# Two places of a twelve-sublayer kernel: four PSUM slots handed out by expected release, and one batch of keys made a stage early

## The reference

```python
for i in range(DEPTH):                                            # 6
    x = attn_layer(shift_tokens(x), Wqkv[i], q_scale[i], k_scale[i], Wo[i]) + x
    x = ffn_layer(shift_tokens(x), ln_g[i], ln_b[i], W1[i], b1[i], W2[i], b2[i]) + x
# attn_layer: q, k, v = x @ Wqkv; q, k l2-normed, scaled, rotated; softmax over 64 keys; @ Wo
# ffn_layer: layer norm, a * gelu(gate), W2
```

```python
h = _mha(x, x, x, Wq1, bq1, Wk1, bk1, Wv1, bv1, Wo1, bo1, causal=True)
out = _mha(h, encoder_k, encoder_v, Wq2, bq2, Wk2, bk2, Wv2, bv2, Wo2, bo2, causal=False)
# _mha: q = x @ Wq + bq, k, v alike; softmax(q k^T / sqrt(8)) v; @ Wo + bo
```

## Time and profile before

| | us |
|---|---|
| median of 3 runs | 4151.44 (4146.84 to 4154.14) |
| the profiled execution, its own time | 4158.42 |
| its span, first to last instruction | 4156.6 |
| local transformer, from 2440 to 3405 | 965 |
| first attention of the double one, from 3464 to 3579 | 115 |
| second attention, from 3579 to 4094 | 515 |

### The profile page before, as it was taken

One profiled execution on the slowest core, in us unless ns is written; L12 is line 12 of the kernel. 1 busy time (PEld: TensorE's weight loads), 2 busy tenths in 40 slices (PEclk: granted clock), 3 DMA queues, 4 the chain that ended last, 5 costly groups with the idle time before them and its releaser, 6 DMA issues. The chain is left out here.

```text
span 4156.6 us, 96204 instructions
## 1 busy us (share of the span) xinstructions
PE 3506.0 (84%) x40492; PEld 2405.1 (58%) x40492; DVE 2612.0 (63%) x4495; ACT 1970.9 (47%) x3518; POOL 1271.6 (31%) x844
## 2 busy tenths in 40 slices
PE   7575888999999996799778668888888878799996
PEld 4455656777777776433232446666666656466674
DVE  5124485666666663688775857777777757556563
ACT  1132345555555553588711235555555544255552
POOL 1102205555555544100030445555555521000000
PEclk9586799999999997999889779999999999699996
DMA  1022300000000006200001021111111101000000
GB/s 39 5 68 74 124 27 11 9 1 9 1 1 1 1 1 210 95 1 1 4 1 44 24 71 42 34 46 52 34 46 36 27 17 36 12 17 19 11 2 11
DMA packets 88438, 131.27 MB, mean 32 GB/s; under 512 B 18290, under 2 KB 59946, under 8 KB 87244
## 3 DMA queue, kind: packets, MB, share of 16 engines
q1 hardware_dynamic: 85004, 118.89, 10.1%
q0 software_dynamic: 3008, 6.23, 0.4%
HBM read 86.37 MB, written 10.94 MB: 23 GB/s over the span
## 5 line engine op out<-in xcount | busy, mean ns | idle before, releaser
L2196 ACT ACTIVATE narrow_probsT<-narrow_ps_t 128x512 f32<-128x512 f32 (+1 forms) x448 | 233.3, 568 | 224.9 <-PE narrow_ps_t L2110 222.4
L2686 POOL TENSOR_TENSOR wide_probs<-wide_probs,wide_factor 128x1024 f32<-128x1024 f32 x128 | 239.7, 1894 | 311.5 <-ACT wide_factor L2647 311.5
L175 POOL TENSOR_TENSOR model_Y<-model_Y,model_X 128x512 f32<-128x512 f32 x12 | 15.2, 1269 | 1029.7 <-POOLq L66 1029.7
L2643 ACT ACTIVATE wide_probs<-wide_ps_s,wide_nm 128x1024 f32<-128x1024 f32 (+1 forms) x256 | 237.7, 929 | 172.2 <-DVE wide_nm L2728 152.7
L3098 PE MATMUL bonds_ps<-bonds_act_of,bonds_out 128*32 128x448 f32 (+3 forms) x1024 | 284.3, 573 | 25.1 <-ACT bonds_rows L3081 18.6
L2248 DVE TENSOR_REDUCE narrow_part<-narrow_ps_s 128x1 f32<-128x512 f32 x384 | 236.1, 685 | 105.1 <-PE narrow_ps_s L2093 105.1
L3808 POOL TENSOR_TENSOR local_turn<-local_turn 128x1024 f32<-128x1024 f32 x96 | 226.4, 2367 | 225.9 <-DVE local_turn L3866 225.9
L2110 PE MATMUL narrow_ps_t<-narrow_Q,second_KQ 32*128 32x256 f32 (+1 forms) x1664 | 291.5, 410 | 3.0 <-ACT narrow_probsT L2196 3.0
L2093 PE MATMUL narrow_ps_s<-second_KQ 32*128 32x512 f32 x768 | 255.7, 674 | 35.0 <-DMA second_KQ<-narrow_close 16.9
L2723 DVE TENSOR_REDUCE wide_nm<-wide_ps_s 128x1 f32<-128x1024 f32 x128 | 156.0, 1219 | 193.7 <-PE wide_ps_s L2529 193.7
L3047 DVE TENSOR_TENSOR bonds_strain<-peri_in_moved 128x1664 f32<-128x1664 f32 (+3 forms) x128 | 257.5, 2088 | 7.0 <-ACT bonds_act_of L3070 6.0
(11 more groups left out here) (629 smaller groups left out, 8412.9 us busy)
## 6 DMA issues: line engine op xcount, KB each, us to landing
moe_w<-in_L_ffn_w SPq DMA_DIRECT2D x62, 512.0 KB
local_V<-local_V SPq DMA_DIRECT2D x96, 128.0 KB
e_wqkv<-in_L_ffn_qkv SPq DMA_DIRECT2D x6, 1536.0 KB, 7.3
local_V<-local_V SPq DMA_DIRECT2D x144, 64.0 KB
context_rows<-in_ctx SPq DMA_DIRECT2D x8, 768.0 KB
e_keys<-in_ctx_T SPq DMA_DIRECT2D x6, 800.5 KB, 4.5
second_KQ<-narrow_close SPq DMA_DIRECT2D x64, 58.0 KB
e_source<-in_ctx_T SPq DMA_DIRECT2D x4, 800.5 KB, 4.4
```

What stands on the lines that cost most here:

```text
L2196: act.activation(probsT[0:high, c % PROBS, h, 0:wide], bank[0:high, 0:wide], ACT.Exp).then_inc(t_taken_act.sem, 1)
L2643: act.activation(probs[:, n % 2, h, lo:hi], ps_s[h][:, 0:hi - lo], ACT.Exp, bias=nm[:, n % 2, h, 2 * half:2 * half + 1], scale=1.0, accum_ ...
L2686: pool.tensor_tensor(v, v, factor[:, n // 4 % 2, j:j + 1].broadcast_to([P, CUT]), ALU.mult).then_inc(lowered[i].sem, 1)
```

## The change

Two edits that don't touch each other.

In the local transformer a slot is chosen by a small plan: with a guess of how long PE makes each kind (`MAKES`) and how long its reader holds it (`HOLDS`), each unit takes the slot that comes free first, and waits for that slot's last user (`last_in`). DVE's sum of the probabilities becomes an event "inv" of its own, behind v (gv) and ahead of s.

In the double attention the keys of batch 0 of the second part are made in steps 6 to 9 of the first, one piece a step ("ahead"), and spread by SP behind them. Its queries of batch 0 are no longer packed and spread: four products with weights that the host has already padded to the spread layout ("query", 256 columns each) give them, and ACT writes them into `KQ`. The padded weights lie in the tile `O`, which isn't in use yet. SP's first reload of the context waits for nothing but its reading, and DVE's start waits for `top` alone (in all three calls of the function).

```diff
@@ early_narrow
+        early.close = early.sbuf("close", [P, K + T])
+        early.O = early.sbuf("O", [P, 2, TB, D])
+        early.first_q = early.O[:, :, :, :].rearrange("p k t d -> p (k t) d")
+        early.load(early.first_in, early.first_q, m.dram[a.name + "_first_q"])
+        early.load(early.first_in, early.first_cols[:, :], m.dram[a.name + "_first_cols"])
@@ narrow_attention, the order
+    AHEAD = (6, 7, 8, 9)
+    AHEAD_UNITS = [(0, 512), (512, 1024), (1024, 1536), (1536, S)]
...
-                for n in range(len(project_units)):
-                    put(N * s - (8 * (len(project_units) - n) + 12 if s else 18 - 4 * n), 7, "project", s, n)
+                for n in range(2 if s == 0 else 0):
+                    put(N * s - (18 - 4 * n), 7, "query", s, n)
+                for n in range(len(project_units) if s else 0):
+                    put(N * s - (8 * (len(project_units) - n) + 12), 7, "project", s, n)
...
+            if following is not None and s in AHEAD:
+                events.append((at, 3.5, "ahead", s, AHEAD.index(s)))
@@ SP
+                side, nth = taken_t(("ahead", AHEAD[-1], len(AHEAD) - 1))
+                sp.wait_ge(side.sem, side.nth(nth))
+                for g in range(G):
+                    for h in range(H):
+                        at = DH * (H * g + h)
+                        sp.dma_start(following.KQ[32 * h:32 * h + DH, 0, g, 0:S], following.close[at:at + DH, 0:S]).then_inc(following.first_K_in.sem, 16)
...
+                sp.wait_ge(source_read.sem, source_read.nth(1))
+                sp.dma_start(source[:, 0, :], m.dram["ctx_T"][2]).then_inc(source_in[0].sem, 16)
+                for b in range(1, B):
@@ POOL
             pool.memset(top[:, :, :, :], 0.0)
+            pool.drain().then_inc(top_cleared.sem, 1)
@@ PE
+                if kind == "ahead":
...
+                    pe.matmul(bank[:, 0:c1 - c0], following.qk[:, 0, P:], following.source[:, 0, c0:c1], start=True, stop=True).then_inc(made.sem, 1)
+                elif kind == "query":
...
+                    for j in range(2):
+                        mm = pe.matmul(bank[:, j * T:(j + 1) * T], early.first_q[:, 2 * n + j, :], qsrc[:, 0:T], start=True, stop=True, skip_group_check=True)
...
-                        pe.wait_ge(KQ_in[b % 2].sem, KQ_in[b % 2].nth(0, b // 2 + 1))
+                        wait_keys(pe, b)
+                        if b == 0:
+                            side, nth = taken_t(("query", 0, 1))
+                            pe.wait_ge(side.sem, side.nth(nth))
@@ ACT
+                    act.activation(following.close[:, c0:c1], bank[:, 0:c1 - c0], ACT.Identity, bias=following.cols[:, 1:2]).then_inc(t_taken_act.sem, 1)
...
+                        ins = act.activation(KQ[:, 0, i, K:], bank[:, j * T:(j + 1) * T], ACT.Identity, bias=early.first_cols[:, i:i + 1], scale=-scale)
@@ DVE
-            dve.wait_ge(cleared.sem, cleared.nth(1))
+            if a.context:
+                dve.wait_ge(early.first_in.sem, early.first_in.nth(32))
+                dve.tensor_scalar(early.first_cols[:, :], early.first_cols[:, :], -scale, None, ALU.mult).then_inc(scaled.sem, 1)
+            dve.wait_ge(top_cleared.sem, top_cleared.nth(1))
@@ local_layers, rounds(): odd and even round
-                            ("root", r), ("v", r), ("gv", shift), ("s", r - 1), ("rest", r), ("wo", r - 3), ("o", r - 2), ("gx", shift)]
+                            ("root", r), ("v", r), ("gv", shift), ("inv", r - 2), ("s", r - 1), ("rest", r), ("wo", r - 3), ("o", r - 2), ("gx", shift)]
...
-                            ("s", r - 1), ("rest", r), ("wo", r - 3), ("o", r - 2), ("sh", (r - 4) // 2)]
+                            ("inv", r - 2), ("s", r - 1), ("rest", r), ("wo", r - 3), ("o", r - 2), ("sh", (r - 4) // 2)]
@@ local_layers, slots
+    MAKES = {"q": 2, "k": 2, "v": 2, "kt": 1, "qt": 1, "pt": 1, "ot": 1, "s": 1.5, "o": 1.5, "wo": 2, "gm": 0.5, "gv": 0.5, "ga": 2, "gb": 1, "gd": 1.5}
+    HOLDS = {"q": 4, "k": 4, "ga": 4, "gb": 2}
...
+    for e in units:
+        k = min(range(SLOTS), key=lambda k: free[k])
+        clock = max(clock, free[k]) + MAKES[e[0]]
+        free[k] = clock + HOLDS.get(e[0], 1)
+        slot_of[e], turn_of[e] = k, len(users[k]) + 1
+        last_in[e] = users[k][-1] if users[k] else None
...
-            r = rank[e]
-            if r >= SLOTS:
-                wait_taken(pe, units[r - SLOTS])
-            return ps[r % SLOTS], made[r % SLOTS]
+            if last_in[e] is not None:
+                wait_taken(pe, last_in[e])
+            return ps[slot_of[e]], made[slot_of[e]]
@@ DVE
-                elif kind == "exp":
+                elif kind == "inv":
```

More of the change, by code:

```diff
@@ L1897, in narrow_attention @@
     S_KINDS = ("scores", "lift", "value", "divide", "gather", "final")
-    T_KINDS = ("project", "turned")
+    T_KINDS = ("project", "turned", "ahead", "query")
     s_units = [e for e in plan if e[0] in S_KINDS]
@@ L1916, in narrow_attention @@
         KQ = early.KQ if a.context else place.sbuf("KQ", [P, RING // SETS, SETS, W])
-        close = place.sbuf("close", [P, W]) if a.context else None
+        close = early.close if a.context else None
         Q2 = place.sbuf("Q2", [P, RING, T])
@@ L1929, in narrow_attention @@
         inv = place.sbuf("inv", [P, TB, H])
-        O = place.sbuf("O", [P, 2, TB, D])
+        O = early.O if a.context else place.sbuf("O", [P, 2, TB, D])
         OT = place.sbuf("OT", [P, T])
@@ L1939, in narrow_attention @@
         source_read = place.counter("source_read")
+        top_cleared = place.counter("top_cleared")
         cleared = place.counter("cleared")
@@ L1985, in full_t, with wait_keys @@
             return ps_t[r % TBK]
+        def wait_keys(engine, b):
+            if b == 0:
+                engine.wait_ge(early.first_K_in.sem, early.first_K_in.nth(16 * 16))
+            else:
+                engine.wait_ge(KQ_in[b % 2].sem, KQ_in[b % 2].nth(0, (b + 1) // 2))
         def part_of(h):
@@ L2163, in _ @@
             act.wait_ge(loaded.sem, loaded.nth(LOADS))
-            act.wait_ge(scaled.sem, scaled.nth(1))
+            act.wait_ge(scaled.sem, scaled.nth(2 if a.context else 1))
             for e in plan:
@@ L2168, in _ @@
                 b, g = s // G, s % G
-                if kind == "project":
+                if kind == "ahead":
+                    bank = full_t(act, e)
+                    c0, c1 = AHEAD_UNITS[n]
+                    act.activation(following.close[:, c0:c1], bank[:, 0:c1 - c0], ACT.Identity, bias=following.cols[:, 1:2]).then_inc(t_taken_act.sem, 1)
+                elif kind == "query":
+                    bank = full_t(act, e)
+                    for j in range(2):
+                        i = 2 * n + j
+                        ins = act.activation(KQ[:, 0, i, K:], bank[:, j * T:(j + 1) * T], ACT.Identity, bias=early.first_cols[:, i:i + 1], scale=-scale)
+                    ins.then_inc(t_taken_act.sem, 1)
+                elif kind == "project":
                     bank = full_t(act, e)
@@ L2173, in _ @@
                     if a.context and n == 0 and b:
-                        act.wait_ge(KQ_in[(b - 1) % 2].sem, KQ_in[(b - 1) % 2].nth(0, (b + 1) // 2))
+                        wait_keys(act, b - 1)
                     i = g % (G // SETS)
@@ L3507, in local_layers @@
     side_rank = {e: sum((f[0] in BY_DVE) == (e[0] in BY_DVE) for f in units[:i + 1]) for i, e in enumerate(units)}
+    slot_of, turn_of, last_in = {}, {}, {}
+    free, users = [0.0] * SLOTS, [[] for _ in range(SLOTS)]
+    clock = 0.0
+    for e in units:
[4 more added lines that the diff above has]
+        last_in[e] = users[k][-1] if users[k] else None
+        users[k].append(e)
     def last_round(g):
@@ L3563, in wait_made @@
         def wait_made(engine, e):
-            r = rank[e]
-            engine.wait_ge(made[r % SLOTS].sem, made[r % SLOTS].nth(r // SLOTS + 1))
+            k = slot_of[e]
+            engine.wait_ge(made[k].sem, made[k].nth(turn_of[e]))
         def full(engine, e):
             wait_made(engine, e)
-            return ps[rank[e] % SLOTS]
+            return ps[slot_of[e]]
         def wait_taken(engine, e):
@@ L3914, in _ @@
                     dve.wait_ge(gelu_ready.sem, gelu_ready.nth(2 * n + 1 + (kind == "gb")))
-                    slot = ps[rank[e] % SLOTS]
+                    slot = ps[slot_of[e]]
                     for j, f in enumerate((0, 1) if kind == "ga" else (2,)):
```

20 lines of the change are left out of this document (17 added, 3 removed).

## The result

| | before | after |
|---|---|---|
| median of 4 runs each on one chip, us | 4149.57 | 4049.76 (4035.98 to 4052.0) |
| ratio | | 0.9751, 95% interval 0.9727 to 0.9775 |
| profiled execution, span | 4156.6 | 4046.8 |
| local transformer | 988.8 | 896.7 (-92.1) |
| first attention of the double one | 123.8 | 129.9 (+6.1) |

A forecast was written before the change was run, and what follows sets the result against it. PE, the local transformer's fullest engine, waits for DVE's last q or k reading; the second attention's head waits for the DMA spread. 61 + 18.0 - 1 = 78 us off 4158.42 gives 4080.4, less 7.0 profiling excess 4073; range 4050 to 4120.

The forecast's parts named there:

- The two slot waits go: Local transformer: ga's wait in even rounds (1.51 us) and pt's in odd ones (1.84 us) behind q(r) go.
- the forecast's signs of being wrong: Local transformer: two rounds over 38 us, PE waiting for DVE at new units, or DVE busy unbroken from q to s.
- v is the new late one, 0.5 us: Local transformer, even rounds: v takes qt's slot and waits for ACT's copy of qt; 0.5 us taken.
- 2.7 us in 38.74: Local transformer: net gain per two rounds, 3.3 - 0.5 - 0.1 = 2.7 us of a 38.74 us period.
- 22.5 pairs at one price, and "85.2 if none does" as the upper bound: Local transformer: 22.5 pairs of rounds x 2.7 = 61 us; at most 85.2 us if no wait comes back elsewhere.
- The rule on the clock: Head of second attention: idleness throttles PE, so closing the gap brings 2.4 GHz to first scores; 5 us, 4068, 6%.
- inv costs 0.1 us and brings what the walk says of q's reading: Local transformer: inv ahead of s on DVE delays s 0.3 us in even rounds, 0.1 counted; DVE reads q earlier.
- The slower rival (inv on the path): Local transformer: inv delays s, adding 48 x 1.54 = 74 us, if DVE's idle time there falls below 1.54; 4208, 4%.
- The head, -18.0: Head of second attention: first scores come at 3584.0 and not at 3602.03, 18.0 us gained.
- The first attention, +1 between 0 and 5.1: First attention: early key products and ACT's reads cost 1 us, between 0 if hidden and 5.1 if in line.
- the likeliest case, 4059 to 4089: Whole kernel: 45 to 75 us gained from the local transformer, giving 4059 to 4089; chance 58%.
- all of the slot waits are won: Local transformer: rival in which all 85.2 us of slot waits are gained, giving 4049; chance 12%.

The follow-up runs named there:

- kernel 5: Kernel before with the planned slots alone, then ga's and pt's old waits for q's reading given back on PE; 4145.00 us, ratio 0.9985.
- kernels 2: Kernel before with inv's place on DVE alone moved, ahead of s, slots in turn as before; 4087.92 us, ratio 0.9889.
- kernel 8: Changed kernel with each early unit of keys moved next to the q and k products of its step; 4052.87 us, ratio 0.9755.
- kernel 9: Kernel before with a one-column product between two heads' scores in steps 6 to 9 of the first attention; 4236.71 us (one run).

## Why the prediction was right or wrong

- **The two slot waits go**: right. 85.2 us of waits for q's last reading became 1.2. At gd the walk found no wait; there are 7.0 us in 13 waits. That is one of the forecast's signs of being wrong, and so is DVE in the odd round shown, where nothing idles it from q to s (DVE's timeline from 2905.20 to 2915.39). Both came, and the kernel was faster than forecast: they showed an inexact walk, not a lost gain.
- **v is the new late one, 0.5 us**: right in kind and size, 0.25 us in most pairs and 0.94 in some, 8.2 in all.
- **2.7 us in 38.74**: too small by 0.46. At the full clock a pair went from 38.45 to 35.29. The pair chosen had a ga wait of 1.51 us, below the 1.66 of the eleven pairs at full clock. In these the two waits are 3.5 us together and 3.16 were won, so v, gd and inv cost 0.3 us and not the 0.6 set down. 21 x 0.46 = 10 us.
- **22.5 pairs at one price, and "85.2 if none does" as the upper bound**: this step failed. I priced a wait at its own length and one pair at full clock stood for all. 10 of 21 pairs had run in part at 1.2 GHz, nine behind a ga wait and one behind a pt wait, and were 18.5 us longer; some 15 of these no list of waits shows, because they are busy time. The true gain of 92.1 (90 on average over six kernels) is above my bound. The signs were on record: clock 0.97 in the earlier trace rows, and a waits column with 2.5 us as the longest where my pair had 1.84.
- **The rule on the clock**: I weighed it at the head of the second attention, where it gave little, and not in the local transformer, where it gave the largest part of the error, some 15 of 31 us. At the head the forecast held: first scores at 1.2 GHz, DVE unhurried. The clock came back at 3522, ahead of the end of the value products and some 28 us behind the first scores, against 30 us before:

```profile
3520.00:3522.00 2.00, 2.00 (x12) 2.00 (x11) 1.42 (x3) 0.00 (x0) 0.00 (x0) 0.50 0.00 0
3522.00:3524.00 2.00, 2.00 (x13) 1.17 (x13) 1.12 (x3) 0.00 (x0) 0.00 (x0) 0.98 0.00 0
```

- **inv costs 0.1 us and brings what the walk says of q's reading**: its own gain was never stated. Alone it is worth 72.7 us, more than the slots.
- **The slower rival (inv on the path)** did not come, though its point of decision was reached: DVE's idle time ahead of s is gone. The criterion was wrong: DVE idle time before one instruction is not the slack of the path. DVE had been late for q because of inv, and now waits there for ACT (46.6 us in 40 waits, 11.3 in 5 before); with inv moved, alone or with the slots, the stretch became shorter.
- **The head, -18.0**: right. -19.8 in the trace after, and over all kernels 513.2 to 515.8 became 490.8 to 498.5.
- **The first attention, +1 between 0 and 5.1**: wrong, and above its bound. "DVE sets the pace, PE runs ahead" overlooked that PE's scores pass two heads at a time and that the unit parts them: 4 x (1.06 or 0.36 + 0.74) = 6.5 us at full clock. The step that failed is the rate at which it was taken to be hidden; the four steps that hold the units are 6.5 us longer by the trace after. As a whole it went from 123.8 to 129.9, but its length varies from 116.5 to 129.3 us in seven kernels with the same code there.
- **The sum**: 61 became 92 (18 in the low pairs, of which some 15 by the clock, 10 by the pair, 3 in the filling and emptying rounds), 18.0 became 19.8, 1 became 6.1, and 4 us came from elsewhere: 78 became 110 between the profiled executions. The forecast also took 7.0 us of the profiled execution's excess off; by the four times it was 8.8, and the one after is 1.2 below its median, so 32 us of error there are 23 between forecast and median.
- **The rivals**: the likeliest case, 4059 to 4089, didn't come; the time stands at "all of the slot waits are won" (4049, 12%), but by another way: 15 us of new waits at gd and v stand against the 85.2, and clock was won. That it meets this case's time is luck.

## What to carry to other kernels

Before pricing a wait, cut the stretch into its repeats and list length, busy time and granted clock of every one; if the same work is busy longer in some, the waits ahead of it can cost more than their own length, and one clean repeat isn't the average. When two edits aim at one wait, try each alone: the cheap one (here one DVE sum moved) can hold most of the gain. A unit put between products that share the array by rows costs its own time and the overlap it breaks; place it next to a product that uses all rows.

## What the runs showed of the hardware

- Behind a wait of 2.36 us PE ran at 1.2 GHz, behind one of 1.51 us it didn't. No pair without an idle time of 1.8 us ran low (182 pairs), 28 of 35 with one over 2.1 us did. The length of the wait alone doesn't settle it: a pair whose longest wait was 1.96 us ran low in part, and one with a wait of 2.38 us (kernel 5) did not.
- The clock also falls where PE hardly idles. At the end of the first attention it goes to 0.50 in all fourteen profiles; in the trace before PE was busy for 7.3 of the 8 us ahead of that, in the one after for 7.4. But it falls 95 us behind the sublayer's start in the trace before and 111 in kernels 2 and 5, with the same code there, and with it goes the length of the first attention, 123.8 and 116.5 to 116.7 us. In kernel 8 it was low for 24 us with PE busy for 23.96 of them. What sets the moment stays open; no experiment was aimed at it.
- In the trace before, the score products of two heads (32 rows each) and the turned ones beside them pass together in 0.9 us, from 3490.67 to 3491.56, the time that one head takes in kernel 9. There one product of a single column over 128 rows between them costs 1.05 us a step, 0.31 of its own.
